# Attention times v in a fused cross-attention and FFN kernel: probabilities stationary, v streamed

## What is computed

```
q = layernorm(x) @ Wq.T + bq            (16 heads of 8)
k, v = ctx @ Wkv.T + bkv
q, k = rms_norm per head
attn = softmax(q k^T / sqrt(8)) over the 64 context tokens of the batch
x = x + attn @ v
h = layernorm(x) @ w1 + b1, rounded to 1/256, piecewise linear GELU on 32 segments, rounded
out = x + round(h @ w2 + b2)
```

## Time and profile before

| | us |
|---|---|
| median of three runs | 237.03 |
| the profiled execution | 238.52 |
| its span, first to last instruction | 236.7 |
| attention steps, first probabilities to last product | about 28 to 140 |
| one step of the loop | about 7.2 |
| TensorE busy | 183.9 |
| VectorE busy | 192.4 |
| ScalarE busy | 146.5 |
| GpSimd busy | 129.6 |

### The profile page before, as it was taken

How to read it: one execution, slowest core, us unless ns; L and a number is a source line. 1 busy time by engine, 2 the same in 40 slices (tenths; PEclk the granted TensorE clock), 3 DMA queues, 4 the chain that set the end, 5 groups by cost and what they waited for, 6 DMA issues and landing times.

```text
span 236.7 us, 8272 instructions
## 1 busy us (share of the span) xinstructions
PE 183.9 (78%) x3227; PEld 140.8 (59%) x3227; DVE 192.4 (81%) x344; ACT 146.5 (62%) x227; POOL 129.6 (55%) x175
## 2 busy tenths in 40 slices
PE   1177959889888888888887789439999999875562
PEld 0165748767667666676675544237767656645562
DVE  6868886988898888988888458699799999999751
ACT  2123755777667686677685676947787887875001
POOL 4547657586877677877775322326344553465200
PEclk9999976999999999999999999967999999997777
DMA  2441110111001111000000000000101101101011
GB/s 81 120 125 47 47 41 11 47 47 44 18 26 44 44 44 35 11 21 22 4 6 3 3 3 0 1 0 0 44 0 48 44 0 47 44 0 44 0 47 44
DMA packets 14542, 7.46 MB, mean 32 GB/s; under 512 B 1075, under 2 KB 14390, under 8 KB 14521
## 3 DMA queue, kind: packets, MB, share of 16 engines
q1 hardware_dynamic: 14104, 6.97, 10.3%
q10 hardware_dynamic: 416, 0.20, 0.3%
HBM read 5.06 MB, written 2.10 MB: 30 GB/s over the span
## 4 chain that ended last, share of the span: by engine, by line
DVE 30%; POOL 23%; PE 19%; issue 17%; ACT 4%; DVEq 2%; DMA 1%; SPq 1%; POOLq 1%; ACTq 0%
POOL y_raw L399 6%; PE bank_o L1077 6%; DVE xn_all L605 4%; POOL qk_hat L335 4%; DVE act_q L828 4%; DVE frac L807 3%; POOL rstd L313 3%; PE banks_s L1062 3%; DVE g_hi L814 3%; POOL xn L311 3%; POOL rstd L329 3%; DVE y_raw L822 2%; POOL xn L316 2%; PE g_hi L911 2%; DVE stats L594 2%
## 5 line engine op out<-in xcount | busy, mean ns | idle before, releaser
L399 POOL TENSOR_TENSOR y_raw<-g_lo,y_raw 128x1024 f32<-128x1024 f32 x15 | 35.4, 2363 | 38.1 <-DVE frac L807 38.1
L1077 PEld LDWEIGHTS bank_o<-w,act_q 128*128 128x128 f32 x256 | 36.5, 224 | 8.1 <-DVE act_q L828 7.3
L1077 PE MATMUL bank_o<-w,act_q 128*128 128x128 f32 x256 | 37.5, 310 | 3.1 <-DVE act_q L828 3.0
L451 ACT ACTIVATE probs<-banks_s 128x512 f32<-128x512 f32 x64 | 33.0, 602 | 3.1 <-PE banks_s L952 2.5
L1062 PE MATMUL banks_s<-x2T,w 128*128 128x512 f32 x60 | 31.1, 600 | 0.0
L938 PE MATMUL g_hi<-ident,parts 128*128 128x128 f16 x256 | 20.5, 225 | 9.4 <-POOL parts L342 5.8
L342 POOL TENSOR_TENSOR parts<-qk_hat,parts 128x512 f16<-128x512 f32 x16 | 18.6, 1160 | 14.3 <-DVE parts L629 14.3
L441 ACT ACTIVATE partsT<-g_hi 128x1024 f16<-128x1024 f16 x16 | 16.4, 1024 | 14.3 <-PE g_hi L938 14.2
L422 ACT ACTIVATE xcT<-bank_in 128x512 f32<-128x512 f32 x16 | 9.6, 597 | 22.7 <-PE bank_in L898 22.7
L520 ACT ACTIVATE g_hi<-seg,gelu_hi 128x1024 f32<-128x1024 f32 x16 | 17.9, 1118 | 9.3 <-DVE y_raw L822 9.3
L938 PEld LDWEIGHTS g_hi<-ident,parts 128*128 128x128 f16 x256 | 15.2, 100 | 13.8 <-issue 7.4
(11 more groups left out here) (103 smaller groups left out, 413.4 us busy)
## 6 DMA issues: line engine op xcount, KB each, us to landing
x_all<-in_x_dram SPq DMA_DIRECT2D x16, 128.0 KB, 2.3
c_in<-in_ctx_dram SPq DMA_DIRECT2D x16, 128.0 KB, 2.1
out_dram<-x_all SPq DMA_DIRECT2D x8, 256.0 KB, 2.3
w<-in_L_ffn_w_dram SPq DMA_DIRECT2D x2, 256.0 KB
wkv_raw<-in_L_xattn_Wkv_dram ACTq DMA_DIRECT2D x1, 128.0 KB, 2.5
bkv_rep<-in_L_xattn_bkv_dram SPq DMA_DIRECT2D x1, 128.0 KB
wq_raw<-in_L_xattn_Wq_dram ACTq DMA_DIRECT2D x1, 64.0 KB, 2.3
b_rows<-in_L_xattn_bq_dram SPq DMA_DIRECT2D x4, 0.4 KB
```

The lines of the kernel that those rows point to most:

```text
L399: g.tensor_tensor(y_raw[u][:], g_lo[n % 3][:], y_raw[u][:], ALU.add).then_inc(S[f"gelu{u}_done"], 1)
L451: a.activation(probs[i][:].rearrange("p t g n -> p (t g n)"), bank_s(i), ACT.Exp).then_inc(S["probs_ready"], 1)
L1077: last = t_.matmul(out, act_q[u][:, c, P * t:P * t + P], w2[:, CH // UNITS * u + c, :], start=False, stop=(u == UNITS - 1 and t == GT - 1 ...
```

## The change

`times_v` swaps its operands: 64 columns of `probs` are stationary (128 rows, 64 columns), and the 32 columns of the v block are streamed, in two column tiles of the array. The product comes out in token rows, in the places of `bank_o` where `out_back` put them. `copy_outT`, `out_back`, the tile `outT` and their semaphores are gone, and `heads_out` waits for `pv_done` itself.

```diff
-            def copy_outT(s):
-                wait(act, "pv_done", s + 1)
-                wait(act, "out_back", s)
-                a.activation(outT[:].rearrange("p t g n -> p (t g n)"), bank_o[:], ACT.Copy).then_inc(S["outT_copied"], 1)
...
             def heads_out(s):
-                wait(dve, "out_back", s + 1)
+                wait(dve, "pv_done", s + 1)
                 wait(dve, "x1_ready", s)
...
                 for gg in range(2):
-                    for b in range(2):
-                        for i in range(4):
-                            c0 = (2 * t + gg) * P + 64 * b
-                            last = t_.matmul(bank_o[ROWS * i:ROWS * i + ROWS, c0:c0 + 64],
+                    for i in range(4):
+                        for b in range(2):
+                            c0 = (2 * t + gg) * P + ROWS * i
+                            last = t_.matmul(bank_o[64 * b:64 * b + 64, c0:c0 + ROWS],
+                                             probs[i][:, t, gg, 64 * b:64 * b + 64],
                                              v_blk[par][:, 2 * t + b, 2 * i + gg, :, :].rearrange("p h e -> p (h e)"),
-                                             probs[i][:, t, gg, 64 * b:64 * b + 64],
-                                             start=True, stop=True, tile_position=(0, ROWS * i))
+                                             start=True, stop=True, tile_position=(0, 64 * b))
                 if t == 1:
                     last.then_inc(S["pv_done"], 1)
-
-            def out_back(s):
-                wait(pe, "outT_copied", s + 1)
-                for a in range(4):
-                    last = t_.transpose(bank_o[:, P * a:P * a + P], outT[:, a // 2, a % 2, :], ident[:])
-                last.then_inc(S["out_back"], 1)
```

More of the change, by code:

```diff
@@ L161, in xattn_ffn @@
         v_blk = [sb(f"v_blk{k}", [P, 4, PAIRS, 2, VW]) for k in range(2)]
-        outT = sb("outT", [P, 2, 2, P])
         den_inv = sb("den_inv", [P, 2 * HEADS])
@@ L200, in xattn_ffn @@
             hi_ready shift_ready lo_ready parts_t parts_t_copied0 parts_t_copied1 scores_ready probs_ready v_proj v_evac
-            pv_done outT_copied out_back den_ready attn_ready x1_ready
+            pv_done den_ready attn_ready x1_ready
             bound_sq_ready g_done g_loaded g_stats g_moments g_var g_rstd g_centred g_xn g_in_t g_in_copied
@@ L459, in step @@
                     rms(s + 1)
-                if runs(s - 1, STEPS):
-                    copy_outT(s - 1)
                 if runs(s + 2, STEPS):
@@ L556, in _ @@
             copy_x2(0)
-            copy_outT(last - 1)
             round_first(0)
@@ L561, in _ @@
             round_first(1)
-            copy_outT(last)
             a.preload_act_table(ACT.Gelu)
@@ L995, in step @@
                     scores(s, 1)
-                if runs(s - 1, STEPS):
-                    out_back(s - 1)
                 if runs(s + 2, STEPS):
@@ L1112, in _ @@
             hidden_first(1)
-            out_back(last_step - 1)
             for t in range(2):
@@ L1119, in _ @@
             transpose_x2(1)
-            out_back(last_step)
             hidden(1, 0)
```

## The result

The changed kernel takes 245.31 us, the median of four runs from 243.94 to 245.77. The kernel before, on the same chip, took 237.17 (234.72 to 238.63). The ratio is 1.0365, with a 95% interval of 1.0299 to 1.0431: slower by 3.7%. The profiled execution took 245.77 us at a span of 243.9, 7.25 us above the 238.52 of before. The forecast was 241.7 with 235.5 to 245.5 around it; 237.03 x 1.0365 = 245.7 lies just above that. The direction was right, the size was too small.

What follows compares the result with a forecast made beforehand. The bound was a closed chain, lows, transposes, times_v, bias_v, normalise, scale_q, cast, with 0.68 us slack a step. Terms 2.6 + 0.3 + 0.9 + 0.8 = 4.6 us on 237.03 gave 241.7 us, range 235.5 to 245.5.

Steps and rivals of the forecast that it cites:

- The cost of `times_v`: The 64 loads of times_v take 1.87 us against 0.94, at a pitch of 27.5 ns: +0.92 us a step.
- Rival 1: In times_v streaming sets the pitch, nothing is added, only the removals' gains remain: 235.8 us; chance 0.12.
- rival 2: In times_v loads are not hidden under products, pitch 41 ns, 1.75 us added a step: 253 us; chance 0.04.
- rival 3: In times_v partial overlap, pitch 17 to 25 ns, the loop hides all: about 237.8 us; chance 0.10.
- The loop: Loop and straight steps, 11 turns: each grows by 0.92 - 0.68 = 0.24 us, together +2.6 us.
- The removals in the loop: Copies and transpositions removed in the loop: worth nothing, covered by ScalarE's 1.01 us idle and VectorE's order.
- Step 14: bias_v already waits for TensorE by 0.33 us, so all of the longer times_v counts: +0.9 us.
- The early step: TensorE is behind there: removing out_back gives -0.7, the longer times_v +1.0, together +0.3 us.
- The last step: times_v(15) starts 0.1 earlier but takes longer, delaying ScalarE's copy at 142.36 on which the FFN hangs: +0.8 us.
- Rival 4: Clock drops in the loop; a half-clocked times_v adds up to 1.9 us in each step concerned; chance 0.02.
- d: Time the new times_v adds a step, forecast +0.92 us; at 0.25 (3d = 0.7) the gain is used up.

Runs made afterwards that it cites:

- e4_half_stream: The changed kernel with each times_v product streaming 16 of the 32 v block columns from step 1 on; measured once, 242.94 us.
- e3_quarters: The changed kernel with probs cut into 32 stationary columns in four column tiles, 128 loads and products instead of 64; 239.71 us, ratio 1.0139.
- e2_order: The changed kernel with normalise put ahead of bias_v on VectorE; 242.48 us, too scattered for a ratio.
- e6_removal: The kernel before without copy_outT and out_back, times_v operands not exchanged, attention output changed in meaning; 236.64 us, ratio 0.9985.
- e5_operands: The kernel before with only the times_v operands exchanged, copy_outT and out_back kept, attention output changed in meaning; 248.2 us, ratio 1.0511.
- e1_fill: The changed kernel with scores(14, 0) issued five times and transpose_x2(0) four times as small filler products; 245.65 us, ratio 1.0367.
- e7_wide_fill: The changed kernel with wide filler products, 12 of 256 columns in step 14 and 4 of 512 before transpose_x2(0); 240.76 us, ratio 1.0211.
- e8: The changed kernel with times_v in four column tiles of 32 stationary columns plus the wide filler products; 239.67 us, ratio 1.0143.
- e11: The changed kernel with normalise ahead of bias_v plus the wide filler products; 239.61 us, ratio 1.0108.
- e12: The changed kernel with normalise ahead of bias_v, wide filler products, and 32-column quarters in the last three times_v only; 240.13 us, ratio 1.0117.
- e9_before_wide: The kernel before with the wide filler products in the same two places, as a control; 235.23 us, ratio 0.9954.

## Why the prediction was right, and where it was not

**The cost of `times_v`.** Right. Forecast: pitch 27.5 ns, a burst of 1.87 us. Measured: 1.95 us for 64 loads, a pitch of (1950 - 143) / 63 = 28.7 ns, so +1.0 us instead of +0.92. That the loads set it was an inference from the slope of the earlier trace rows; e4_half_stream shows it, with half the streaming and an unmoved burst, and so does e3_quarters, with twice the products in 0.76 us less. Rival 1, that streaming decides, is refuted, and so are rival 2 (41 ns) and rival 3 (17 to 25 ns). The Trainium skill (TensorE: Matmul & The Clock Gate, LDWEIGHTS) counts columns over 1.2 for a load, 53 ns here. Halved for two tiles that is an estimate of 27 ns; the measured 28.7 is near it. Its floor of about 25 ns between starts of products (same page, "Wait — 56ns, not 53.3ns?") does not hold across column tiles: e3_quarters has 128 products in 1.30 us, at most 10.2 ns apart.

**The loop.** Right in mechanism and in size: 7.47 us a step in mean where 7.45 was forecast, `bias_v` 0.11 us behind the last product, `scale_q` waiting for `normalise`, +2.86 us over 11 turns for +2.6. e2_order shows that the place is `bias_v` before `normalise`: exchange them and the step is 7.23. The removals in the loop gave nothing, as forecast; e6_removal shows it for the old operands. For the new ones the removal gave 0.15 us a step (e5_operands), inside a sum in which it was already counted.

**Step 14.** Right: +0.93 for +0.9.

**The early step.** Wrong in sign in the two profiles, -0.77 instead of +0.3, and neither confirmed nor refuted as a forecast. The gain of 0.7 us and the loss of 1.0 were worked out for a step at half clock (before's window from 34 to 37 us has 0.50). In the execution after that step ran at full clock, and an earlier one ran slowly instead (`project_qk` at 27 us, above). The same kernel code reached `lows(3)` at 43.45 us in after, at 41.74 in e1_fill and at 41.58 in e7_wide_fill, so where the stretch at half clock falls moves this term by more than the change was said to. No profile has this step of before at full clock.

**The last step.** Wrong, and the largest term of the miss: "all of the FFN hangs on that copy ... +0.8", measured +4.24. The chain named there was right: with the clock held the stretch grew by 0.67 us and the way to that copy by 0.81 (e7_wide_fill). What failed is the assumption under it, that TensorE works at full clock at the seam from attention to the FFN. The sum has no term for it. Rival 4 took the clock for granted because "TensorE streams less but is not idle longer", looked for a drop in the loop alone, and gave it 0.02. In the loop it stayed at 1.00, as said. At the seam, where TensorE already stood in two gaps of 1.35 and 0.94 us before, these grew to 1.49 and 1.24, with less work between them since `out_back(13)` was gone, and the clock fell for about ten microseconds. That cost 3.57 us in the profile. e5_operands shows that it isn't the missing `out_back` alone, and e7_wide_fill that it is TensorE's lack of work there: filling the same gaps with work of no use keeps the clock. The other profiles say the same. All six with the new operands and no wide products (after, e1 to e5) have windows at half clock between 128 and 143 us, and all four with the wide products (e7, e8, e11, e12) have 1.00 there.

So the +7.26 are 2.86 + 0.93 + 0.67 = 4.5 us of longer loads, near to the forecast's 4.6, and 3.57 us of clock, less 0.77 early. That the 4.5 and the 4.6 lie so near is in part luck, since the 4.6 has an early term of +0.3 and the 4.5 has none.

One point of the prediction's working does not fit the rest. Rival 1 puts the turning point at d = 0.25, where 3d uses up the early gain of 0.7 us, but the same rival counts 0.5 us more at the end; with both the point is 3d = 1.2, d = 0.4. The measured d of 1.0 is far above either.

**What stays open.** What exactly makes the clock fall at this seam in one execution and not in another: e6_removal had one such window, before had none in its profile, and each kernel has one trace only. Whether some executions of before lose the clock here too, as the gain of e9_before_wide might mean, was not seen. Also where the long gaps put down to "issue" come from (2.07 us in e1_fill, 0.89 in e8_quarters_fill); they appeared with bursts of more than a hundred small TensorE instructions, and their cause wasn't tried.

## What to carry to other kernels

When two operands are exchanged, price the loads apart from the streaming: columns of the stationary side over the number of column tiles in use gave the pitch here, and the exchange that saved a copy and four transpositions, both off the path, doubled a burst that was on it. Then look past the loop: the places where TensorE already stands idle for a microsecond at a time are where a small delay can be multiplied, since the clock may fall there, for ten microseconds in this case. A few wide products with no use, put into such a gap, are a cheap test: here they gave back 3.57 us in the profile of the changed kernel. Run the same filler in the kernel before as a control, as e9_before_wide does, and read the gain in the stretch where the filler stands; whole times also hold what the clock did elsewhere.

## What the runs showed of the hardware that I had not expected

Adding work made a kernel faster: 16 wide products, 2.5 us of TensorE's time, took the changed kernel from 245.31 to 240.76 us, and 3.57 us of it are seen where they stand. The same idea with 140 small instructions gave nothing (245.65) and a stall of 2.07 us with no visible releaser. The granted clock shown for a window can be 1.00 while equal products run at the length of the half clock (0.63 us for 0.39, at 27 us in after), so early stretches want both readings. Loads in four column tiles overlap, 8.5 ns apart, but they need twice the instructions, and together with the filler that gave up what the loads gained. And a transposition and a copy of 512 columns a step, sixteen times over, were worth nothing within the measurement (0.9985 [0.9936, 1.0035]).
